# Lookup operands of the edge sort on all 128 partitions, zero below row 25

## The reference

```python
h = jnp.maximum(_layernorm(x, axis=-1), 0.0)
x = x + _L0_gnn_ref(h, edge_index, edge_attr_18, ...)    # attention, sums over src
h = jnp.maximum(_layernorm(x, axis=-1), 0.0)
x = x + _L1_gnn_ref(h, edge_attr_64, edge_weight, edge_index, ...)  # attention, sums over dst
h = jnp.maximum(_layernorm(x, axis=-1), 0.0)
x = x + _L2_gnn_ref(h, ..., src, dst, edge_type_8)       # relation matrices
h = jnp.maximum(_layernorm(x, axis=-1), 0.0)
x = x + _L3_gnn_ref(h, src, dst, ...)                    # attention, sums over dst
```

## Time and profile before

| what | us |
| --- | --- |
| median of three runs | 8772.91 |
| lowest and highest of them | 8761.85, 8773.75 |
| the profiled execution's own time | 8768.56 |
| its span, first to last instruction | 8766.8 |
| TensorE busy in the span | 6632.5 (76%) |
| VectorE busy | 5350.9 (61%) |
| GpSimd busy | 5210.0 (59%) |
| ScalarE busy | 3574.4 (41%) |
| mean granted TensorE clock | 0.781 |

### The profile page before, as it was taken

The page is one execution under the profiler, slowest core; times in us unless marked ns, Lnnn a source line. Parts: engine busy times, 40 slices in busy tenths (PEclk is TensorE's granted clock), DMA queues, the critical chain, the costliest instruction groups (busy, mean ns, idle before and its releaser), DMA issues. The chain is left out here.

```text
span 8766.8 us, 144073 instructions
## 1 busy us (share of the span) xinstructions
PE 6632.5 (76%) x33110; PEld 4747.4 (54%) x33111; DVE 5350.9 (61%) x15337; ACT 3574.4 (41%) x10757; POOL 5210.0 (59%) x5090
## 2 busy tenths in 40 slices
PE   5999998999979898956777777578655554576765
PEld 5777775666656666643555555464343342444444
DVE  4677776666657777775999999511222223455556
ACT  2322222333357666733666665123000001577772
POOL 0377776777767677713777776000577771577771
PEclk9655555555589999988999999688777776788887
DMA  8311111111145555523666665002444441344442
GB/s 263 81 17 17 17 17 26 33 33 34 33 116 141 136 138 140 138 61 112 184 176 177 171 178 157 31 10 90 117 108 108 108 108 30 89 109 109 109 109 46
DMA packets 1016911, 849.18 MB, mean 97 GB/s; under 512 B 755122, under 2 KB 845025, under 8 KB 1012783
## 3 DMA queue, kind: packets, MB, share of 16 engines
q0 software_dynamic: 257152, 645.64, 27.1%
q1 hardware_dynamic: 713513, 154.62, 8.9%
q10 hardware_dynamic: 45780, 44.08, 1.4%
HBM read 723.28 MB, written 120.67 MB: 96 GB/s over the span
## 5 line engine op out<-in xcount | busy, mean ns | idle before, releaser
L1108 POOL DMA_INDIRECT edges_kv<-kv,edges_rec x1712 | 1998.1, 1167 | 956.8 <-issue 504.4
L1218 PE MATMUL banks<-edges_kv,edges_hot 128*128 128x288 f32 (+2 forms) x5136 | 1548.2, 451 | 646.5 <-DVE edges_kv L1464 439.7
L1218 PEld LDWEIGHTS banks<-edges_kv,edges_hot 128*128 128x128 f32 x5136 | 1037.4, 212 | 1021.2 <-issue 585.0
L1619 POOL DMA_INDIRECT edges_rows<-rel,edges_rec x856 | 811.4, 948 | 980.0 <-DMA edges_rec<-by_dst_records 723.3
L1108 POOL DMA_INDIRECT edges_kv<-feat,edges_rec x856 | 834.6, 975 | 484.7 <-issue 253.8
L542 POOL DMA_INDIRECT by_src_records<-sort_by_src_rec,sort_pos_i x808 | 776.5, 961 | 578.7 <-issue 573.5
L671 PE MATMUL banks<-sort_table,sort_hot_hi_t 25*128 25x128 f32 x3232 | 951.8, 444 | 51.3 <-DVE sort_junk L612 46.3
L1635 PE MATMUL banks<-edges_rows,edges_hot 128*128 128x256 f32 x1712 | 625.8, 530 | 468.1 <-DMA edges_rows<-rel,edges_rec 445.0
L542 POOL DMA_INDIRECT by_dst_records<-sort_by_dst_rec,sort_pos_i x808 | 776.3, 961 | 285.8 <-issue 244.1
L1453 DVE TENSOR_TENSOR acc<-edges_pair_sums,acc 128x288 f32 (+2 forms) x1284 | 562.2, 438 | 496.1 <-DMA edges_kv<-feat,edges_rec 291.1
L671 PEld LDWEIGHTS banks<-sort_table,sort_hot_hi_t 25*128 25x128 f32 x3232 | 721.2, 307 | 220.4 <-issue 121.1
(11 more groups left out here) (359 smaller groups left out, 12587.9 us busy)
## 6 DMA issues: line engine op xcount, KB each, us to landing
edges_kv<-kv,edges_rec POOLq DMA_INDIRECT x1712
sort_feat<-in_edge_attr_dram SPq DMA_DIRECT2D x100, 256.0 KB, 3.7
rel<-tables_stage SPq DMA_DIRECT2D x25, 1008.0 KB
by_dst_records<-by_dst_blank ACTq DMA_DIRECT2D x1, 17120.0 KB, 100.1
edges_rec<-by_dst_records SPq DMA_DIRECT2D x107, 160.0 KB
edges_rows<-rel,edges_rec POOLq DMA_INDIRECT x856
edges_kv<-feat,edges_rec POOLq DMA_INDIRECT x856
by_src_records<-sort_by_src_rec,sort_pos_i POOLq DMA_INDIRECT x808, 2.1
```

The source lines that it names most:

```text
L1108: pool.indirect_dma_start(kv[:, r, c, 0:koff + DIM], None, tab, bass.IndirectOffsetOnAxis(ap=reci[:, r, c, idx:idx + 1], axis=0)).then_inc ...
L1218: last = pe.matmul(ps[:, 6 + m % 2, 0:OW], hot[:, b % 2, c, :], kv[:, b % BUFS, c, koff:koff + OW], start=(c % 2 == 0), stop=(c % 2 == 1))
L1619: pool.indirect_dma_start(rows[:, b, c, :], None, tab, bass.IndirectOffsetOnAxis(ap=reci[:, b, c, idx:idx + 1], axis=0)).then_inc(gathered ...
```

## The change

Both lookup operands become tiles of 128 partitions. GpSimd fills them with zeros once in the first block, ScalarE still writes their first 25 partitions, and the line of the lookup product is unchanged: its `hot_hi_t[:, u, c, :]` and `table[:, d % 2, :]` now take 128 rows, of which 103 hold zero.

```diff
-        hot_hi_t = ph.sbuf("hot_hi_t", [NB, 2, G, P])
+        hot_hi_t = ph.sbuf("hot_hi_t", [P, 2, G, P])
...
-        table = ph.sbuf("table", [NB, 2, P])
+        table = ph.sbuf("table", [P, 2, P])
...
                 pool.iota(duo_i[:], pattern=[[DUO, T // 2]], base=0, channel_multiplier=0).then_inc(filled, 1)
+                pool.memset(table[:], 0.0).then_inc(filled, 1)
+                pool.memset(hot_hi_t[:], 0.0).then_inc(filled, 1)
                 for K in keys_of:
                     pool.memset(K.seg_prev[:], 0.0).then_inc(filled, 1)
...
-                    act.copy(table[:, 0, :], starts[:]).then_inc(table_ready, 1)
+                    act.copy(table[0:NB, 0, :], starts[:]).then_inc(table_ready, 1)
...
-                        act.copy(hot_hi_t[:, b % 2, 4 * h:4 * h + 4, :], ps[0:NB, 0, :].rearrange("k (c e) -> k c e", c=4)
+                        act.copy(hot_hi_t[0:NB, b % 2, 4 * h:4 * h + 4, :], ps[0:NB, 0, :].rearrange("k (c e) -> k c e", c=4)
...
-                            act.copy(table[:, (d + 1) % 2, :], ps[0:NB, TABLE, 0:P]).then_inc(table_ready, 1)
+                            act.copy(table[0:NB, (d + 1) % 2, :], ps[0:NB, TABLE, 0:P]).then_inc(table_ready, 1)
```

## The result

The changed kernel takes 8746.28 us (median of eight runs, 8721.54 to 8754.52); the kernel before, in the runs beside it, 8772.85 (eight runs, 8761.85 to 8782.81). The ratio is 0.9968, with a 95% interval of 0.9957 to 0.9978: faster by 0.22 to 0.43%. The forecast of 8758 and the range from 8750 were too high. The profiled execution, the fastest of the eight, took 8721.54 us, with a span of 8719.8.

A forecast was written before the change was run, and what follows sets the result against it. GpSimd was taken to bound the second pass, and a close race with the TensorE and VectorE chain the first. 8768.56 - 9.7 - 2 x 0.5 = 8757.9, rounded to 8758 us; own range 8751 to 8765, 8 in 10 from 8750 to 8773.

The forecast's parts named there:

- rows count as activity: TensorE in both scatter passes: few-row products don't count as full activity; with zeros, mean clock 0.6 to 0.9.
- clock stays: Rival, both scatter passes: TensorE stays at 0.50, passes keep 1045.8 and 1034.2 us, time 8768.6; chance 0.17.
- small waits: First pass: GpSimd waits a little for late positions, steps 10.31 against 10.12 us; priced -9.7 us, bounds 0 and -11.6.
- long pauses: GpSimd, seven in each pass, 2.24 us in the first, mostly shorter in the second; some 1.9 us together, not credited.
- The race of a step: First pass: 10.12 us of GpSimd against 10.31 us of the TensorE and VectorE chain in each step.
- the second pass in 1034 as before: Sign to look for: GpSimd's DMAs of the second pass still run from first to last in 1034 us.
- GpSimd's cadence is not fixed: Sign against the forecast: both passes under 1030 us would mean GpSimd's 1.265 us per indirect DMA isn't fixed.
- lead-ins: Pass start to first indirect DMA, 15.3 us with GpSimd idle; priced -0.5 us each, bounds 0 and -2.5.
- more than the step race: Rival: early high clock wins 2.5 us before each pass's first DMA and shortens first-pass pauses; 8752 us, chance 0.08.
- the product's price: Lookup products of both passes: 128 rows cost the same as 25; 0 taken, other bound some 5 ns a record.
- dearer lookup: Rival: 128 rows lengthen each lookup, deciding from 22 ns; at 43 ns, 35 us in the first pass, 8804; chance 0.05.
- VectorE's wait: First pass: VectorE's 189.5 us of waiting for the lookups of line 671 should fall below 100.

The follow-up runs named there:

- the halved projection: Kernel before without the second half of the contraction in the projection beside the second pass; second pass 1028.8 us, against 1032.2 with it.
- the repeat on one chip: Changed kernel and kernel before run again without edits on the same chip; medians 8756.93 against 8774.36 us, ratio 0.9983.
- the run meant to tell: Changed kernel run once more, no edit, on a chip where the kernel before takes 10508.05 us; ratio 0.9998 (0.9975 to 1.002).

## Why the prediction was wrong, step by step

**Right: rows count as activity.** The clock rose from 0.50 to 0.77 with 128 rows, stayed with 32, and stayed in the first pass with 64; added full products raised it under unchanged lookups (0.59). The rule of the Trainium skill, "TensorE: Matmul & The Clock Gate", section "What's actually happening", which goes by how busy TensorE was lately and names no rows, doesn't agree with what the traces show: TensorE at 94% busy kept 0.50, and with zeros below the same products it got 0.77 at 73%. The rival "clock stays" is refuted. One detail of my reading was wrong: the stretch right before 1910 isn't the one with 0.42 but one with 0.71 busy and a clock of 0.90.

**Right: GpSimd becomes the bound of both passes**, and more TensorE work is then free. The size of the small waits was about right: 9.7 forecast, with 11.6 as the bound, and 11.2 us measured in the first pass on one chip. The second pass lost another 1.9 of such waits, which I had at nothing.

**Wrong: the long pauses.** The race of a step was read rightly, but the sum was too small: 10.7 us against 22.9 in the traces of one chip. The largest part of that is one term, "together some 1.9 us that I have no reason to give to TensorE", which I had put at nothing. It measured 3.7 us in the first pass and 1.9 in the second, 5.6 in all. I had seen that the pauses had two lengths in the earlier trace rows, 2.24 and 1.85, and took the second pass as the floor. It was itself a pass with a nearly late chain: with other work taken away (the halved projection) its pauses fell to 1.76. So 1034 us was no floor either. "the second pass in 1034 as before" fell for the same reason, and "GpSimd's cadence is not fixed" was the wrong sign to look for: the 0.30 us between DMAs kept, and the seven pauses moved.

**Too small: the lead-ins.** Priced at 0.5 us each, bounds 0 and 2.5; they gave 2.2 and 2.0, of which 2.0 each from the first table copy on (15.4 to 13.4, 16.7 to 14.7). The clock rose at 313 us, 5 us before the first DMA, not only at the end. I had put the first burst behind most of the lead-in. The rival "more than the step race" had both terms, 8752, with a chance of 0.08. It was the nearest; its 16.6 us plus the 3.8 that the second pass lost are 20.4, near the measured 22.9.

**Right: the product's price.** The shortest record of a lookup is 269 ns with 25 rows and 274 with 128 on one chip; 5 ns a record was the bound that I had named. My way to it proved nothing, though: I took the price of a record and the tail from the same two rows, and from two rows such a price and tail can always be found. What supports the price is the comparison of the shortest records. The dearer lookup (22 ns) didn't come. The fills cost nothing visible: the first DMA comes earlier.

**Wrong in size: VectorE's wait.** I expected 189.5 us to fall below 100, and over the same stretch, 480 to 1360 us, it reads 150.8. In a step bound by GpSimd each engine with slack idles somewhere; VectorE's idle time stayed at the lookups, since it waits there in the order of its program. A wait by an engine with slack says little of what it costs.

**Open: the rest.** The median of the first result is 26.6 us below its runs of before, that of the repeat on one chip 17.4, and the traces account for 22.9 in the latter. In the profile of the first result the stretch behind the passes was also shorter, 6316.1 us against 6335.9. Its GpSimd DMAs are a few ns faster, as on other chips with the kernel before; nothing links this to the change, and the run meant to tell fell on the chip of 10508 us. The other traces speak for chance: that profile is of the fastest execution of eight, and in the thirteen other profiles on ordinary chips the stretch behind the passes takes 6331 to 6348 us, with the change (6347.8, 6338.7, 6331.4) as without it (6335.9, 6339.6). My sum was 10.7 us; since it started from an execution 4.3 us below the median of before, the forecast time itself missed by 11.7. Some 12 of the difference to the first result are explained by pauses (5.6), lead-ins (3.2) and small waits (3.4); about 4 are not.

## What to carry to other kernels

A product with few rows cost the same time as a full one here, to 5 ns a record, and can keep the clock down for its whole stage; try zeros below it before trying to make it shorter. When two stages share a bound, don't take the better one as the floor: check whether it too is close to waiting, by taking some other work away. Price a step that adds work at the clock that the work brings about, not at the one in the trace.

## What was not expected of the hardware

- More work made a stage shorter: eight more 128-row products in each step took the first pass from 1045.9 to 1033.8 us by a clock of 0.59 in place of 0.50.
- GpSimd pauses after every 112 indirect DMAs of these passes, nearly always for 1.70 to 2.24 us. The length went with how far the other engines were ahead and not with TensorE's clock: 1.71 to 1.76 us in a pass at 0.52, 2.24 in one at 0.64.
- A lead-in stayed at 0.50 for 18 us although TensorE was busy for 91% of 303 to 319 us, added full products among it, while the same lead-in without them reached 1.00 at 315.
- A one-row product (two records, together 0.7 us) in each of the 25 groups of the two-layer network costs the stage 12 us, most of it by the clock: 232.9 to 220.5 us with 128 rows in its place.
